# Attention's projection stage: two utok buffers, transposes two tiles later, and ScalarE's norm of a tile one tile later

## The reference

```
def _L1_attn_ref(x, Wq, Wk, Wv, Wo, xsa_scale):
    q, k, v = (proj(Wq), proj(Wk), proj(Wv))       # 16 heads of 64
    scores = jnp.einsum('bhqd,bhkd->bhqk', q, k) * SCALE
    attn = jax.nn.softmax(scores, axis=-1)
    out = jnp.einsum('bhqk,bhkd->bhqd', attn, v)
    dot = jnp.sum(out * v, axis=-1, keepdims=True)
    v_norm_sq = jnp.sum(v * v, axis=-1, keepdims=True) + EPS
    out = out - xsa_scale * (dot / v_norm_sq) * v
    return jnp.einsum('bsd,ed->bse', out, Wo)
```

## Time and profile before

| | |
|---|---|
| median of 3 runs | 5106.56 us (5091.76, 5106.56, 5410.48) |
| the profiled execution | 5103.29 us |
| its span, slowest core (6) | 5101.9 us |
| spans of the 8 cores | 5055.0 to 5101.9 us |
| TensorE busy | 4316.6 us (85%) |
| VectorE busy | 2330.5 us (46%) |
| ScalarE busy | 2287.7 us (45%) |
| GpSimd busy | 275.1 us (5%) |

### The profile page before, as it was taken

One profiled execution on the slowest core, in us unless ns is written; L12 is line 12 of the kernel. 1 busy time (PEld: TensorE's weight loads), 2 busy tenths in 40 slices (PEclk: granted clock), 3 DMA queues, 4 the chain that ended last, 5 costly groups with the idle time before them and its releaser, 6 DMA issues.

```text
span 5101.9 us, 73795 instructions; the slowest of 8 cores (5055.0 to 5101.9 us)
## 1 busy us (share of the span) xinstructions
PE 4316.6 (85%) x27136; PEld 2055.3 (40%) x27136; DVE 2330.5 (46%) x3228; ACT 2287.7 (45%) x2843; POOL 275.1 (5%) x457
## 2 busy tenths in 40 slices
PE   3897886689888898856799897669989979999999
PEld 2776775334333444422222222232222234444444
DVE  2667884022114433433344443333434447677676
ACT  3665653243233222311488785119878812222221
POOL 0001121110011111100000000000000000000000
PEclk9999997899999999978999998889999979999999
DMA  7444555765466544630000002200010051111110
GB/s 158 146 149 145 177 156 139 237 205 156 138 199 227 176 148 151 198 107 25 21 1 26 34 28 76 75 29 1 17 34 26 30 194 42 42 52 42 42 52 34
DMA packets 204455, 502.05 MB, mean 98 GB/s; under 512 B 24775, under 2 KB 24903, under 8 KB 204105
## 3 DMA queue, kind: packets, MB, share of 16 engines
q1 hardware_dynamic: 144634, 302.26, 18.5%
q0 software_dynamic: 59472, 195.06, 13.2%
HBM read 390.30 MB, written 125.83 MB: 101 GB/s over the span
## 4 chain that ended last, share of the span: by engine, by line
PE 73%; DMA 10%; DVE 7%; DVEq 3%; issue 3%; another core or an unknown queue 1%; ACT 1%; ACTq 0%; SPq 0%; POOL 0%; POOLq 0%
PE ps L1599 9%; PE ps L1629 9%; PE ps L952 9%; PE ps L1298 7%; PE ps L480 6%; PE ps L1285 6%; DMA w1r<-s_w1t 6%; PE ps L906 4%; PE ps L1302 4%; PE ps L1257 4%; PE ps L1361 3%; PE ps L1246 2%; PE ps L945 2%; PE ps L1328 2%
## 5 line engine op out<-in xcount | busy, mean ns | idle before, releaser
L1394 ACT ACTIVATE Pr<-ps,shc 128x1024 bf16<-128x1024 f32 x1024 | 1108.9, 1119 | 157.6 <-PE ps L1285 108.1
L906 PE MATMUL ps<-xnB,w1r 128*128 128x512 bf16 x2048 | 504.8, 399 | 140.3 <-DMA w1r<-s_w1t 128.0
L999 ACT ACTIVATE hT<-ps,b1c 128x512 bf16<-128x512 f32 x256 | 175.6, 687 | 783.6 <-PE ps L906 783.0
L1645 ACT ACTIVATE h<-z 128x512 bf16<-128x512 f32 x256 | 161.3, 630 | 702.7 <-DVE z L1668 702.6
L1599 PE MATMUL ps<-u,q 128*128 128x512 bf16 x2048 | 467.2, 382 | 10.4 <-DVE z L1668 5.5
L1298 PE MATMUL ps<-Pr,vk 128*64 128x512 bf16 x2048 | 417.7, 404 | 64.2 <-DVEq L1464 64.2
L1629 PE MATMUL ps<-u,q 128*128 128x512 bf16 x2048 | 447.2, 379 | 0.0
L952 PE MATMUL ps<-w2t,hT 128*128 128x512 bf16 x2048 | 447.2, 379 | 0.0
L1285 PE MATMUL ps<-qT,kT 64*128 64x512 bf16 x2048 | 401.2, 387 | 12.1 <-ACT Pr L1394 2.5
L1302 PE MATMUL ps<-Pr,onesb 128*64 128x512 bf16 x2048 | 394.9, 381 | 0.0
L906 PEld LDWEIGHTS ps<-xnB,w1r 128*128 128x128 bf16 x2048 | 199.5, 101 | 386.4 <-issue 199.1
(11 more groups left out here) (185 smaller groups left out, 5795.3 us busy)
## 6 DMA issues: line engine op xcount, KB each, us to landing
wna<-L_ffn_W POOLq DMA_DIRECT2D x128, 512.0 KB, 4.9
w1r<-s_w1t SPq DMA_DIRECT2D x256, 256.0 KB, 7.0
wnb<-L_ffn_W POOLq DMA_DIRECT2D x128, 512.0 KB, 7.8
xt<-x_in SPq DMA_DIRECT2D x16, 1024.0 KB, 9.0
xr<-x_in SPq DMA_DIRECT2D x32, 512.0 KB, 9.1
s_x<-xr SPq DMA_DIRECT2D x32, 512.0 KB, 2.6
xk<-s_xn SPq DMA_DIRECT2D x16, 1024.0 KB, 5.6
xh<-s_x SPq DMA_DIRECT2D x64, 256.0 KB, 2.7
```

The lines of the kernel that those rows point to most:

```text
L906: mm = t.matmul(o, K.w1r[h % R1][:, j * P:(j + 1) * P], xb[:, :, j, :], start=j == 0, stop=j == 7)
L1394: a.activation(K.Pr[i % NP][:], bank(K, 2 * (i % 2), 2), AF.Exp, bias=K.shc[:], scale=0.125).then_inc(S.a_ex, 1)
```

## The change

The transposes of TensorE stand two tiles behind V instead of one, the last ones after the last Q group; utok has two buffers, taken in turn; ScalarE does the norm of tile T-1 after the K copies of tile T; in VectorE's round utok of tile tl-1 comes ahead of the copy to uT of tile tl-2.

```
-            K.utok = sb("utok", [P, D], BF16, ska)
+            K.utok = [sb(f"utok{i}_", [P, D], BF16, ska) for i in (0, 1)]
...
         mm.then_inc(S.p_h3, 1)
-        if n < 68 and n % 4 == 3 and n >= 4:
-            tl = n // 4 - 1
+        if n % 4 == 3 and n >= 8:
+            tl = n // 4 - 2
             k = K.T0.fill(("u", bi, tl))
             pe.wait_ge(S.t0e, k)
             pe.wait_ge(S.v_ut, 16 * bi + tl + 1)
             ps = t16(K, 6, BF16)
             for j in range(8):
                 mm = t.transpose(ps[:, j * P:(j + 1) * P],
-                                 K.utok[:, j * P:(j + 1) * P], K.ident[:])
+                                 K.utok[tl % 2][:, j * P:(j + 1) * P], K.ident[:])
...
     for n in range(72):
         b, s, g = n // 16, n % 16 // 4, n % 4
+        if n % 4 == 3 and 4 <= n < 68:
+            p3_se_norm(K, bi, n // 4 - 1)
         if n < 64 and g >= 2:
-            if g == 3:
-                tl = n // 4
-                c = slice(16 * (tl % 2), 16 * (tl % 2) + 16)
-                se.wait_ge(S.v_ssq, 16 * bi + tl + 1)
-                a.activation(K.lsq[:, c], K.ssq[:, c], AF.Ln, bias=K.xeps[:])
-                a.drain()
-                a.activation(K.rsv[:, c], K.lsq[:, c], AF.Exp, scale=-0.5).then_inc(S.a_rsv, 1)
             continue
...
+def p3_se_norm(K, bi, tl):
+
+    se, S, a = K.se, K.S, K.nc.scalar
+    c = slice(16 * (tl % 2), 16 * (tl % 2) + 16)
+    se.wait_ge(S.v_ssq, 16 * bi + tl + 1)
+    a.activation(K.lsq[:, c], K.ssq[:, c], AF.Ln, bias=K.xeps[:])
+    a.drain()
+    a.activation(K.rsv[:, c], K.lsq[:, c], AF.Exp, scale=-0.5).then_inc(S.a_rsv, 1)
...
-        if tl >= 2:
-            p3_ve_unit(K, bi, tl - 2)
         if 1 <= tl < 17:
             q = tl - 1
             ve.wait_ge(S.a_rsv, 16 * bi + q + 1)
-            if q >= 1:
-                ve.wait_ge(S.t0, K.T0.at[("u", bi, q - 1)] + 1)
-            v.tensor_tensor(K.utok.ap().rearrange("p (h e) -> p h e", h=16),
+            if q >= 2:
+                ve.wait_ge(S.t0, K.T0.at[("u", bi, q - 2)] + 1)
+            v.tensor_tensor(K.utok[q % 2].ap().rearrange("p (h e) -> p h e", h=16),
                             K.vk[:, q * D:(q + 1) * D].rearrange("p (h e) -> p h e", h=16),
                             K.rsv[:, 16 * (q % 2):16 * (q % 2) + 16].unsqueeze(2).broadcast_to([P, 16, 64]),
                             ALU.mult).then_inc(S.v_ut, 1)
+        if tl >= 2:
+            p3_ve_unit(K, bi, tl - 2)
```

## The result

| | before | after |
|---|---|---|
| runs compared, us | 5091.8, 5106.6 | 4865.8, 4866.6, 4877.0, 4884.5 |
| ratio of their times | | 0.9552 (95% interval 0.9534 to 0.9570) |
| profiled execution, us | 5103.3 | 4865.8 |
| span of the slowest core, us | 5101.9 | 4864.4 |
| TensorE busy, all stages | 4316.6 us (85%) | 4253.0 us (87%) |

The changed kernel is 4.5% faster; its median is 4871.8 us.

The account below looks back on a forecast made before the run. The projection stages were taken as bound by a chain of waits, TensorE idling until VectorE's utok. Savings of 115.1 and 112.4 us in the two sequences, 227.5 off 5103.3, gave 4876 us, range 4860 to 4900.

Parts of the forecast that it names:

- The stage: First V matmul to first score matmul: 129.3 us in the first sequence instead of 244.4; 7.4 us a tile.
- The split into waiting and clock: Of the gain in the projection stages, about 70% is waiting removed and 30% TensorE's higher clock.
- ScalarE's norm: Norm one tile later, after the kT copies: ScalarE doesn't wait, rsv at 5.3 us, VectorE asks at 10.7 us.
- The ends: Last transposes behind the last Q group, their eviction before attention: last Q to first score 0.93 us becomes 1.0.
- Rival 1: Projection stages: a bank freed late by VectorE or ScalarE stops TensorE once a tile; 4907 to 4948 us, chance 0.08.
- Rival 2: TensorE's clock stays at 0.82 when all cores project without pauses; 56 us given back, 4932 us, chance 0.04.
- Rivals 3 and 4: Only half the utok wait goes, 4990 us, chance 0.02; short bank stops keep the clock low, 5133 us, 0.01.
- The room: VectorE may be 1.4 us late at the first V copy; bank 6 is free with 2.2 us to spare.
- What lies outside the stages: Attention and all later stages don't change and only start earlier; 227.5 us come off the 5103.3 us execution.
- The wait: Projection stage: TensorE idles 78.7 us before the transposes until VectorE's utok, 5.3 us a tile; the change removes it.
- The two buffers: Two utok buffers, with 2.8 us of room, cited against the case that only half the wait goes.

Follow-up runs that it names:

- e10: Kernel before, with 20 filler matmuls ahead of both waits of the transposes (bank 6 and utok): 5049.3 and 5057.5 us, ratio 0.9887 of before.
- e1: Changed kernel with ScalarE's norm back at its old place, before the next tile's K copies: 4908.3 and 4921.6 us.
- e11: Kernel before, with only ScalarE's norm moved as in the change: 5102.6 to 5135.3 us, ratio 0.9995 of before.
- e8: Changed kernel with the squares computed three times in each VectorE round (2.6 us more): 4893.9, 4896.3 and 4908.0 us.
- e2: Changed kernel with VectorE's old order, eviction to uT ahead of utok: one comparable run, 4894.8 us, stage 129.1 us.
- e6: Kernel before, with only VectorE's order changed, utok ahead of the eviction to uT: 5104.3 to 5115.4 us, ratio 0.9978 of before.
- e3: Changed kernel with a single utok buffer: 4870.8, 4871.1 and 4878.2 us, stage 129.1 us.
- e9: Kernel before, norm moved as in the change, utok first in VectorE's round, transposes still one tile behind, one buffer: 4874.7 to 4876.4 us, ratio 0.9560.
- e5: Kernel before, with 20 filler matmuls between the transposes' waits for bank 6 and utok: one comparable run, 5199.9 us.

## What held in the prediction, and which of its steps failed

The forecast of 4876 us stands beside a median of 4871.8, and the saving of 227.5 us beside 228, the mean of 5099.2 of the two runs of before times 0.0448. That the total is off by 4 us only is in part luck, as the four runs after differ by 19 us. The mechanism of the sum held: the wait for utok went, the clock came up, and nothing took their place. The steps that failed stand beside that sum; they come behind the list.

- **The stage.** Forecast 129.3 us, measured 129.1 on every core; 7.4 us a tile, measured 7.35. The sum is this close because its two terms, the eight-matmul group and the set of transposes, were both read where TensorE isn't stopped, and because nothing else of the stage came on the path.
- **The split into waiting and clock.** About 70 to 30 by the sum, 74 to 26 by e10. The step held; e10 is what turns it from a calculation into a measurement.
- **ScalarE's norm.** "ScalarE doesn't wait at all, and rsv is there": in the tiles between, it is as read (rsv 5.2 us after V ended, utok's start 10.8). The last tile is an exception that the prediction didn't look at: its norm stands behind three Q copies, and VectorE waits 1.8 us for rsv, in both sequences, with no stop of TensorE after it. That a norm in front of the kT copies holds V is shown by e1, and that its place is worthless as long as utok holds the transposes by e11.
- **The ends.** The last eviction to uT came onto the chain, 0.93 us becoming 2375.47 - 2374.54 = 0.93, so it cost nothing more; what moved onto the path is the last set of transposes, which the 16 sets in the sum hold.
- **Rival 1** isn't what happened. Its price, 1.1 us a tile and more, is somewhat above that of e1 and e8, 0.98 and 0.79 us a tile, which show how near such a kernel lies.
- **Rival 2** is out: the clock is 1.00 with all cores in the stage at nearly the same time. The Trainium skill's rule (TensorE: Matmul & The Clock Gate, "Part 1: The HAM clock gate"), 13/16 of the clock for a die from its third core with dense matmuls on, isn't borne out by this trace: the stage shows 1.00 on all four cores of each die.
- **Rivals 3 and 4** are out, with idle time before the transposes gone and the clock at its upper level.

**The steps that failed.** None of them takes the time out of the forecast, and no run ties a miss of the total to one of them. As far as the runs show, the clearest is the room.

- **The room, mis-sized and at the wrong place.** "VectorE may be late by 1.4 us before anything stops" took the bank of the first V copy for the one that stops TensorE first, and left out that VectorE idles before that copy (0.59 us in the timeline after). By e8 the room is 1.8 us a tile, and the one that stops TensorE is bank 6, through the eviction at the end of the round, to which the prediction had given 2.2 us.
- **What lies outside the stages, put at nothing.** "Attention and all later stages don't change and only start earlier", and the sum takes 227.5 us off one execution. Between the profiled executions went 237.5 us: 228.1 in the two stages and 9.4 outside them, 7.7 of these ahead of the first stage. In the same code a core begins that stage anywhere from 2205 to 2254 us before, and one of e2 at 2272. No run shows what sets this, so the cause stays open.
- **The wait, put down to utok alone**, as the profile names the last to come. The eviction that frees bank 6 ended at 2301.07, only 1.1 us before utok at 2302.21, and both waits had to go; e6 shows that moving utok ahead gains nothing, with the wait at 5.39 us until the eviction.
- **The two buffers, taken as part of what keeps the distance of two tiles** ("Against it are the two buffers"). By e3 one is enough.

## What to carry to other kernels

Where a fast engine waits in each round for a chain through others, take a product that they have had a round's time to make, by a longer distance or by the order in which they work (e9), and check every queue that the chain passes: here the norm's place was worth almost nothing alone and 17 to 20 us a stage once the longer wait was gone. Price the stage after the change from rows where the bounding engine isn't stopped; that counts the clock too, a quarter of this gain. Before adding a buffer, compare the time of the write with that of the last read.

## What the runs showed of the hardware

Work that computes nothing made the kernel 1.1% faster (e10), by keeping TensorE's granted clock at its upper level (2.4 GHz; 0.99 and 1.00 on average in the two stages) through waits of 5.3 us. Behind the wait for bank 6 the same work made it some 2% slower (e5). And with waits in the stage the clock differed by core: before, cores 0 and 1 needed 255.7 and 254.2 us for the first stage, where the others needed 242.5 to 244.7, in the same code and with the same 78.7 us of waiting. On core 0 the mean clock of this window was 0.73 instead of 0.82:

```profile
2254.00:2480.00 226.00, 150.25 (x576) 64.61 (x576) 77.98 (x85) 26.48 (x61) 0.00 (x0) 0.73 0.07 23
```

In e11 it was again two cores, 2 and 3, with 254.4 and 253.7 us. With no waits this spread is gone, 129.1 us on all cores. Why two cores got the lower level for longer is open.
